# Row maxima of two heads side by side in a transformer block with cross and self attention

## What is computed

```python
q = (layernorm(x) @ wq.T + bq); k = (ctx @ wk.T + bk); v = (ctx @ wv.T + bv)
out = softmax(q @ k.T / 4) @ v                   # 16 heads, cross attention
x = x + tanh(g0) * out
# layer on layernorm(x): rotary self attention with 16 heads of the same kind,
# rmsnorm, a shared feed-forward net, two of eight routed experts, rmsnorm
x = x + tanh(g1) * layer(layernorm(x))
```

## Time and profile before

| | |
|---|---|
| median of three runs | 869.47 us (867.1 to 869.69) |
| the profiled execution | 871.39 us |
| its span, first to last instruction | 869.7 us |
| mean granted TensorE clock | 0.939 |
| TensorE busy | 775.3 us, 89% |
| VectorE busy | 539.6 us, 62% |
| ScalarE busy | 415.9 us, 48% |

### The profile page before, as it was taken

The page is one execution under the profiler, slowest core; times in us unless marked ns, Lnnn a source line. Parts: engine busy times, 40 slices in busy tenths (PEclk is TensorE's granted clock), DMA queues, the critical chain, the costliest instruction groups (busy, mean ns, idle before and its releaser), DMA issues.

```text
span 869.7 us, 10573 instructions
## 1 busy us (share of the span) xinstructions
PE 775.3 (89%) x3606; PEld 353.7 (41%) x3606; DVE 539.6 (62%) x801; ACT 415.9 (48%) x760; POOL 194.2 (22%) x338
## 2 busy tenths in 40 slices
PE   4979999999997997998998799989999289989994
PEld 3522334234232332343234234246446164448883
DVE  3488884875878877777786887703382003452664
ACT  2627787787764773765575476851210022122000
POOL 3330123123123122013102201001017740000454
PEclk9969999999998998999799899988999579999998
DMA  6671233434415323411530521050003633000010
GB/s 196 179 201 47 65 110 127 95 108 148 105 53 151 75 56 116 104 38 49 134 73 1 154 68 35 2 194 2 0 10 118 218 132 109 1 0 2 25 41 33
DMA packets 51573, 73.33 MB, mean 84 GB/s; under 512 B 7232, under 2 KB 42560, under 8 KB 51520
## 3 DMA queue, kind: packets, MB, share of 16 engines
q1 hardware_dynamic: 47936, 63.93, 26.4%
q0 software_dynamic: 3072, 8.46, 2.7%
q10 hardware_dynamic: 512, 0.26, 0.1%
HBM read 45.04 MB, written 27.33 MB: 83 GB/s over the span
## 4 chain that ended last, share of the span: by engine, by line
PE 67%; DVE 14%; ACT 6%; issue 5%; DMA 2%; POOL 2%; SPq 1%; ACTq 0%; DVEq 0%; POOLq 0%
PE ps L1330 32%; PE ps L1448 11%; PE ps L1468 10%; PE ps L1420 9%; DVE negm L1006 5%; PE ps L1325 2%; DVE qk L931 2%; ACT hS L791 2%; ACT rows L718 1%; DMA w<-scrk 1%; DVE bst L910 1%; PE ps L1436 1%; PE ps L1428 1%; DVE qk L970 1%; ACT oT L698 1%
## 5 line engine op out<-in xcount | busy, mean ns | idle before, releaser
L1006 DVE TENSOR_REDUCE negm<-ps 128x2 f32<-128x1024 f32 x256 | 302.1, 1222 | 52.1 <-PE ps L1420 47.1
L791 ACT ACTIVATE hS<-ps 128x512 f32<-128x512 f32 x512 | 274.9, 599 | 107.5 <-PE ps L1468 105.7
L1420 PE MATMUL ps<-w 96*128 96x512 bf16 x512 | 163.1, 402 | 18.5 <-DVE hS L1025 11.3
L1468 PE MATMUL ps<-w 98*128 98x512 bf16 x512 | 165.9, 395 | 4.0 <-ACT hS L791 3.0
L1448 PE MATMUL ps<-hS,mix 128*17 128x512 f32 x1024 | 139.9, 619 | 0.2
L1468 PEld LDWEIGHTS ps<-w 98*128 98x128 bf16 x512 | 40.8, 99 | 161.7 <-ACT hS L791 83.6
L1197 DVE SCALAR_TENSOR_TENSOR ctxs<-qk,ps 128x512 f32<-128x512 f32 x32 | 22.0, 688 | 96.1 <-ACT qk L825 94.9
L1420 PEld LDWEIGHTS ps<-w 96*128 96x128 bf16 x512 | 49.1, 101 | 79.7 <-DVE negm L1006 17.0
L825 ACT ACTIVATE qk<-ps 128x512 f32<-128x512 f32 x32 | 19.1, 597 | 96.2 <-PE ps L1330 87.9
L1330 PE MATMUL ps<-w,hS 128*128 x256 | 55.4, 379 | 0.0
L1330 PE MATMUL ps<-fout,hS 128*128 128x256 f32 x128 | 36.2, 427 | 19.5 <-issue 19.4
(11 more groups left out here) (208 smaller groups left out, 907.2 us busy)
## 6 DMA issues: line engine op xcount, KB each, us to landing
w<-scrq SPq DMA_DIRECT2D x32, 384.0 KB, 4.1
scrq<-mix SPq DMA_DIRECT2D x16, 384.0 KB, 3.3
scrk<-mix SPq DMA_DIRECT2D x24, 256.0 KB, 2.2
scrq<-mix SPq DMA_DIRECT2D x24, 256.0 KB, 2.7
w<-scrk SPq DMA_DIRECT2D x32, 192.0 KB, 4.6
w<-scrk SPq DMA_DIRECT2D x32, 128.0 KB, 4.5
w<-in_L_ffn_W_experts_dram SPq DMA_DIRECT2D x8, 512.0 KB, 8.1
mix<-scrf SPq DMA_DIRECT2D x4, 528.0 KB
```

Of the source, the lines that this page charges most:

```text
L791: nc.scalar.activation(prob[:, kt % PROB_SLOTS, s % HG, :], slot_bank(("unit", u)), ACT.Exp, scale=SC).then_inc(s_exp, 1)
L1006: V.tensor_reduce(negm[:, gi % 2, 2 * t2:2 * t2 + 2, h], ps[:, bank:bank + 2, :], AX.X, ALU.max, negate=True).then_inc(s_re, 1)
L1420: last = MM(ps[:, bank + t, :], qs[0:STK, g, h, tt * P:(tt + 1) * P], ks[0:STK, g, h, :], start=True, stop=True)
L1468: MM(take(("unit", u)), ks[:, g, h, kt * P:(kt + 1) * P], qs[:, g, h, :], start=True, stop=True).then_inc(s_sT, 1)
```

## The change

The row maxima get stacks of their own, `mq` and `mk`, in the region of the weights `fin`. They hold two parts of q by two parts of k, 4 x 16 = 64 rows (`MROWS`), with even heads in rows 0 to 63 and odd heads in rows 64 to 127. A fill is now two heads by one tile of 128 queries: two products, one in each half of the rows. It needs six more DMAs for each group, which SP issues ahead of those for `qs` and `ks`, as soon as the maxima of that group in the instance before are done. The fills keep their lead, but both ring halves are filled together at every fourth step, ahead of the value product; VectorE reduces both there. The reduction writes the same `negm` in another order. The wait for `qs` and `ks` moves to the first score of the group. Because the stacks lie in `fin`, its two weights are loaded after the last maxima; the third late weight moves to the first place.

```diff
+    MROWS = MPART * MPART * DH
...
+        mstacks = fin[:].rearrange("p n c f -> p (n c f)").bitcast(BF16).rearrange("p (x g h l) -> p x g h l", x=2, g=NG, h=HG // 2)
+        mq, mk = mstacks[:, 0], mstacks[:, 1]
...
                 for g in range(NG):
                     ge(sp, s_stk[g], (n - 1) * 64)
+                    ge(sp, s_mst[g], (n - 1) * 96)
...
                 for g in range(NG):
+                    ge(sp, s_m2, (n - 1) * NG + g + 1)
+                    for i in range(2):
+                        r = i * MROWS
+                        sp.dma_start(mq[r:r + MROWS, g], head_pair(scrq, 1, MPART * MPART, g, i)).then_inc(s_mst[g], 16)
+                        for t in range(MPART):
+                            r = i * MROWS + t * MPART * DH
+                            sp.dma_start(mk[r:r + MPART * DH, g], head_pair(scrk, 0, MPART, g, i)).then_inc(s_mst[g], 16)
                     ge(sp, s_sT, ((n - 1) * NG + g + 1) * STEPS)
...
+            sp.wait_ge(s_m2, GROUPS)
+            for i, w_ in enumerate((f_in, f_w1)):
+                sp.dma_start(fin[:, i], w_.rearrange("(k p) n -> p k n", p=P)).then_inc(s_wl, 16)
...
             def row_max(q):
-                h, t2 = p // 2, p % 2
+                h2, tt = p // TT, p % TT
...
-                V.tensor_reduce(negm[:, gi % 2, 2 * t2:2 * t2 + 2, h], ps[:, bank:bank + 2, :], AX.X, ALU.max,
+                V.tensor_reduce(negm[:, gi % 2, tt, 2 * h2:2 * h2 + 2], ps[:, bank:bank + 2, :], AX.X, ALU.max,
...
-                        if s % 2 and q < N_PAIRS:
-                            row_max(q)
+                        if s % HG == HG - 1:
+                            for q_ in (q - 1, q):
+                                if q_ < N_PAIRS:
+                                    row_max(q_)
...
             def max_pair(q):
-                    pe.wait_ge(s_stk[g], (gi // NG + 1) * 64)
+                    pe.wait_ge(s_mst[g], (gi // NG + 1) * 96)
                 bank = ring_bank()
-                for t in range(2):
-                    tt = 2 * t2 + t
-                    last = MM(ps[:, bank + t, :], qs[0:STK, g, h, tt * P:(tt + 1) * P], ks[0:STK, g, h, :],
-                              start=True, stop=True)
+                for i in range(2):
+                    r = slice(i * MROWS, (i + 1) * MROWS)
+                    last = MM(ps[:, bank + i, :], mq[r, g, h2, tt * P:(tt + 1) * P], mk[r, g, h2, :], start=True, stop=True)
...
                         if s == 0:
+                            pe.wait_ge(s_stk[g], (n + 1) * 64)
...
-                        if s % 2 and q < N_PAIRS:
-                            max_pair(q)
+                        if h == HG - 1:
+                            for q_ in (q - 1, q):
+                                if q_ < N_PAIRS:
+                                    max_pair(q_)
```

More of the change, by code:

```diff
@@ L332, in flamingo_block @@
         s_stk = [sem(f"stack_loaded{g}") for g in range(NG)]
+        s_mst = [sem(f"maximum_stack_loaded{g}") for g in range(NG)]
         s_vp = sem("values_ready")
@@ L377, in flamingo_block @@
             for s_ in range(STEPS):
-                taken += s_ % 2 and (gi_ * STEPS + s_) // 2 + LEAD < N_PAIRS
+                if s_ % HG == HG - 1:
+                    taken += sum((gi_ * STEPS + s_) // 2 - j_ + LEAD < N_PAIRS for j_ in range(2))
                 if s_ == AT_HEADS and gi_ > 0:
@@ L487, in stack, with head_pair @@
                     sp.wait_ge(s_scr[X], (n + 1) * SCR[X])
+                def head_pair(scr, first, terms, g, i):
+                    h0 = g * HG + i
+                    return scr[par, first:first + terms].rearrange("r (d h) t -> (r d) h t", h=NH)[:, h0:h0 + HG - 1:2]
                 for g in range(NG):
+                    ge(sp, s_m2, (n - 1) * NG + g + 1)
[5 more added lines that the diff above has]
+                            sp.dma_start(mk[r:r + MPART * DH, g], head_pair(scrk, 0, MPART, g, i)).then_inc(s_mst[g], 16)
                     ge(sp, s_sT, ((n - 1) * NG + g + 1) * STEPS)
@@ L502, in _ @@
             late = [
-                (fin[:, 0], f_in.rearrange("(k p) n -> p k n", p=P)),
-                (fin[:, 1], f_w1.rearrange("(k p) n -> p k n", p=P)),
                 (fout[:], f_out.rearrange("(k p) n -> p k n", p=P)),
             ]
-            assert len(late) == N_LATE
+            assert len(late) + 2 == N_LATE
             stack(0)
@@ L514, in _ @@
                 stack(n)
-                if n - 2 < N_LATE:
+                if n - 2 < len(late):
                     d_, s_ = late[n - 2]
```

## The result

The changed kernel takes 900.27 us (median of 4 runs, 896.92 to 901.45), the kernel before 869.58 on the same chip (4 runs, 867.1 to 870.8). The ratio is 1.0342, 95% interval 1.0299 to 1.0385: 3.4% slower, +30.7 us where 14.6 were forecast. The sign is right, the size is off by a factor of two.

A forecast was written before the change was run, and what follows sets the result against it. TensorE was taken to set the pace. Sixteen plain groups +14.4, intervals behind projections -0.4 and -0.8, and the last two +1.4 sum to +14.6 us: the median 869.47 becomes 884, range 866 to 905.

The forecast's parts named there:

- Fills side by side: In each fill, two 64-row products run at once on TensorE: 0.22 us instead of 0.44, -0.44 per stretch.
- A change of form: On TensorE, a stretch has three changes of array form for two: +0.10 us, bounds 0 and 0.2.
- The fills leave the gap: Plain stretch, value product to value product: four scores in a row, the fourth waiting for its bank; 2.94 us against 2.82.
- The turn: Stretch where the maxima are transposed: TensorE waits 0.9 us for VectorE; 4.18 us against 3.68, plus 0.5.
- Plain group: Undisturbed group of four heads: 3 x 0.13 + 0.5 = +0.9 us, 12.15 to 13.05; sixteen of them +14.4.
- The rival in which the halved work counts: Loop groups: neither wait bites, a stretch falls to 2.55 us, a group to 10.9, the whole to 840; chance 0.15.
- The clock rival: Plain groups: TensorE's idling lowers its clock in each third group, some 3 us each; 905 to 910 us; chance 0.10.
- DMAs: Six more loads per group and two late weights in the loop cost 0 us, bounds 0 and +2.
- The first distance: Start of the loop: paced by reductions and by one DMA, so 0 us of change.
- The small terms: Distances with a projection 0; behind them -0.4 (cross attention) and -0.8 us (self attention); last two distances +1.4 together.

The follow-up runs named there:

- e5_order_alone: The kernel before with its 96-row fills, two together behind every fourth step, and no new loads: 906.56 us against 858.53, 1.0562.
- e6_layout_alone: The changed kernel with one fill behind each second step, as before; 64-row products side by side and new loads kept: 858.40 us against 858.53, 0.9993.
- e4_fills_behind_third: The changed kernel with both fills behind the third of four scores instead of the fourth: 875.31 us against 857.76, 1.017.
- e9_spread: The changed kernel, stacks held back group by group until due maxima rows landed, late weights behind the last rows, x and context earlier: 890.77 us against 866.94, 1.0263.
- e8_loads_alone: The kernel before plus only the new DMAs, their data unread, and the two late weights after the last maxima: 890.87 us against 858.53, 1.0377.
- e1_fin_behind_rows: The changed kernel with the two late weights asked for only when the last rows of maxima have landed: 882.72 us against 857.76, 1.0274.

## Why the prediction was right in sign and wrong in size

**Fills side by side: right.** Two products on the two halves start together in bf16 too, and a fill costs 0.22. Beside the loads, for which no plain stretch waits, `e5_order_alone` and after differ in just that: 3.25 against 2.93 us a stretch, -0.32 for the expected -0.44 + 0.10.

**A change of form: right.** It was put at 0.10. `e6_layout_alone` has three more of them in a stretch than before: 2.82 - 0.44 + 3 x 0.10 = 2.68, measured 2.70. The 0.02 more for an exposed weight load stands on no row, and no run shows it.

**The fills leave the gap: right.** Three and one scores, 0.26 us of idle time for ScalarE at each fourth (0.4 forecast), a stretch of 2.93 for 2.94. (Its excess was given as +0.13; 0.12 and 0.02 make 0.14.) That it is the place and not the number of products is shown by `e4_fills_behind_third`: 2.59 to 2.71 with the fills one step earlier.

**The turn: right.** Fill to turn 3.32 us as worked out, the stretch 4.17 for 4.18. The idle time is 0.67 rather than 0.9, since TensorE arrives at the turn later than I had it; VectorE sets the stretch, so that error costs nothing. 26 turns wait, not some 23.

**Plain group: right.** 12.94 for 13.05, 0.79 a group for 0.9. For these sixteen (of 31 distances, not 30) that makes 12.6 us for 14.4. The rival in which the halved work counts is refuted for this order (2.93, not 2.5), and in the old order its stretch would be 2.70. The clock rival is refuted where it was put, in plain groups: their clock stays at 1.00 (381 to 394 us). A clock that fell did come in two places, behind first scores that had waited 2.60 and 1.24 us for something else than the turn, waits that the rival did not contain. The second, in the third of the four distances behind a self attention:

```profile
451.55 1.91 PE L1470 MATMUL ps<-hS,mix 128*17 128x512 f32 x8
```

From 451.5 to 455 the granted clock is 0.51, the lower level, and that distance (15.39 us) is some 1.2 us longer than its wait explains. In three other groups first scores waited 0.94, 1.05 and 1.27 us and the clock stayed at 1.00 (373 to 379, 302 to 308, 527 to 534).

**DMAs: wrong, the step that failed.** The sentence was "The rows of the maxima, on ScalarE's queue, may land later behind them: they have some 2 us of air", and it was closed with 0, bounds 0 and +2. It measured 9.0 - 4 x 0.79 = +5.9 in the four distances behind the self attentions (4.5 of waits, the rest clock) and +4.5 behind the last turn: +10.4 of the 12.2 us by which the loop missed. The air was used up in each of these places.

The first distance, +3.5, is mixed. The forecast had the start as "paced by reductions and by one DMA: 0", and that failed as well. It is the same wait, for rows behind bulk: with the bulk held back it falls to 11.95 us (`e9_spread`). But the order alone already gives +3.1 with the loads of before, since the first turn comes 1.4 us earlier into traffic that was there anyway. The second turn stands at 69.05 before, 70.67 with the order alone and 71.31 in after, and the loads alone, in the old order, give +2.7 (15.23 us in `e8_loads_alone`). Either is enough to bring the wait about; how much of the +3.5 belongs to which stays open.

The term went wrong in two ways. I asked of the late weights only whether they arrive in time (16 us for two loads of 8.0), and not whom their traffic delays; and I set the new loads against their mean share of the loop, 26.4%, where what counts is the share in the microseconds in which the rows travel. These are the two kernels in the stretch around the third wait above, after and then before:

```profile
290.00:305.00 15.00, 12.51 (x81) 3.06 (x84) 10.85 (x13) 10.38 (x21) 1.66 (x2) 1.00 1.01 227
```

```profile
280.00:295.00 15.00, 15.00 (x90) 4.45 (x89) 12.59 (x15) 11.48 (x22) 1.65 (x2) 1.00 0.60 140
```

The same turn stands at 286.7 in before and at 296.36 in after, so the windows are ten us apart. The DMA engines are busy for 1.01 of the time against 0.60. SP's and ScalarE's queues in after say why:

```profile
297.84 0.58 SPq L505 DMA_DIRECT2D fin<-scrq  x1
...
297.40 0.60 ACTq L730 DMA_DIRECT2D w<-mTs  x1
```

The rows (L730) are issued at 297.40 while SP has issued stack after stack since 287. The Trainium skill (DMA: Bandwidth & Descriptors, Issuing engines are not separate DMA queues) says that DMAs of different engines end up on the same 16 DMA engines and interleave there; the trace agrees as far as the rows, on a queue of their own, are late while these engines are busy for 1.01 of the time. That the loads cause it is shown by `e8_loads_alone` (the waits without the order and the form), by `e5_order_alone` (the order without these waits, but for the first) and by `e1_fin_behind_rows` (the wait at the end gone, 4.5 us back). That the four in the middle are of this kind is shown by `e9_spread`, in which they are 12.94. Those two runs, `e1_fin_behind_rows` and `e9_spread`, also settle what these first scores wait for: the weights that the first moves are no stacks, and the second asks for the stacks later and still loses the four waits, so it was the rows.

**The small terms.** Six distances with a projection cost +0.4 each instead of 0, the last two +1.4 each instead of together (the forecast gave that +1.4 without a working), those right behind the projections of the self attentions gave 3.1 back instead of 0.8. With the first turn 1.3 us early and the plain distances 1.3 us better than forecast these sum to about -1.3, which is luck; none of them was tested.

**What stays open.** The kernel before was profiled once only, in an execution 1.9 us above its median. On the chip of `e6_layout_alone` its 858.53 us are 11 less than on its own. What lies behind the loop takes 284.7 to 288.2 us in the four kernels profiled there, against 294.3, so 6 to 10 of the 11 lie there, and an estimated 1 to 5 us may lie in its loop. The 26.8 us are uncertain by as much, and I can say that `e6_layout_alone` equals the kernel before on that chip, not in which part of the kernel its gain of 0.57 a group is lost again.

## What to carry to other kernels

Before work on the busiest engine is halved or moved, look at what it stands in: products inside a gap that another engine's latency makes cost little (0.19 to 0.31 us for two fills with their changes of form, 0.53 outside it), and the order that left the gap, with the wait at the turn that it brought, cost more here (1.36 us a group) than halving them saved (0.57). And a small DMA that someone waits for is to be costed against the bulk that is in flight in its own microseconds, whichever queue issued it; for each load that is moved, ask whose landing it delays before asking whether it lands in time itself. Once the bulk is held back, it has to be spread: held in blocks, or ahead of something else on its queue, waits came up elsewhere in four runs of five, and the fifth kept six of them.

## What the runs showed of the hardware

The two 4 KB DMAs on ScalarE's queue were in place 3.4 us after the turn in `e1_fin_behind_rows`, and let the first score of their group start only 6.4 to 7.9 us after it where SP's loads were in flight (waits of 1.05, 2.60 and 4.84 us). The Trainium skill (DMA: Bandwidth & Descriptors, Queues, rings and completion order) says that each DMA engine takes turns between its queues by packets; no run here shows packets one by one. What the runs show is 3 to 4.5 us of delay for 4 KB.

A standstill of 2.6 us ahead of 588.67 was followed by products at the lower of the two clocks, 1.2 GHz (1.88 us for four scores), until some 595. A wait of 0.67 us in each group was not followed by such a fall (clock 1.00 from 381 to 394). Between them the length of the wait does not tell: the clock fell behind a wait of 1.24 us and not behind one of 1.27 us. Each microsecond of the long wait was thus paid nearly twice: 2.6 us of waiting, 4.5 us lost.

Two 64-row bf16 products on the two halves cost the pitch of one, 0.22 us (two fills with their change of form take 0.54 us, 385.20 to 385.74), so the gain is the full factor of two for the products themselves. Each change of form in between takes back 0.1 us, almost half of what a fill gains.
